# A message-passing kernel: an intermediate goes through DRAM and comes back repeated, two blocks later

## What is computed

```python
s1 = concat(x[src][:, :8], x[dst][:, :8]);  v1 = the 16 vectors of both ends
w  = relu(emb @ fc1_w1 / sqrt(10)) @ fc1_w2 / 4          # 512 weights per edge
s_t, v_t = first layer of s1, v1 with w                  # 8 + 24 values: "v" below
w2 = relu(emb @ fc2_w1 / sqrt(10)) @ fc2_w2 / 4          # 384 weights per edge
scal, gates, vecs = second layer of s_t, v_t with w2
edge_out = concat(tanh(scal), vecs * tanh(gates)) * norm
x = layernorm(x + segment_sum(edge_out, dst))
```

## Time and profile before

| | |
|---|---|
| median of 3 runs | 751.27 us (750.43 to 751.88) |
| the profiled execution | 750.24 us, span from first to last instruction 748.4 us |
| PE busy | 690.1 us (92%) |
| PEld busy | 285.0 us (38%) |
| DVE busy | 691.3 us (92%) |
| ACT busy | 558.7 us (75%) |
| POOL busy | 529.2 us (71%) |
| mean granted clock of TensorE | 0.991 |
| DMA | 28.49 MB, mean 38 GB/s |

### The profile page before, as it was taken

The page is one execution under the profiler, slowest core; times in us unless marked ns, Lnnn a source line. Parts: engine busy times, 40 slices in busy tenths (PEclk is TensorE's granted clock), DMA queues, the critical chain, the costliest instruction groups (busy, mean ns, idle before and its releaser), DMA issues.

```text
span 748.4 us, 19329 instructions
## 1 busy us (share of the span) xinstructions
PE 690.1 (92%) x5998; PEld 285.0 (38%) x5998; DVE 691.3 (92%) x1230; ACT 558.7 (75%) x1279; POOL 529.2 (71%) x656
## 2 busy tenths in 40 slices
PE   0578999999999999999999999999999999999963
PEld 0323434444443443444444344444444444444321
DVE  7578999999999999999999999999999999999983
ACT  2257778887788888877888888888888878788741
POOL 5678787778876887688768876888688877886100
PEclk9999999999999999999999999999999999999997
DMA  4332211121111111121112111211121111111000
GB/s 111 77 91 48 44 31 29 40 46 27 28 42 45 31 28 43 26 46 29 42 26 48 31 42 25 45 29 44 26 48 29 31 36 37 28 27 28 12 1 23
DMA packets 45714, 28.49 MB, mean 38 GB/s; under 512 B 23191, under 2 KB 43833, under 8 KB 45613
## 3 DMA queue, kind: packets, MB, share of 16 engines
q1 hardware_dynamic: 31175, 19.22, 9.8%
q0 software_dynamic: 13312, 6.84, 6.2%
q10 hardware_dynamic: 1126, 1.18, 0.6%
HBM read 22.46 MB, written 4.74 MB: 36 GB/s over the span
## 4 chain that ended last, share of the span: by engine, by line
PE 86%; DVE 5%; issue 2%; ACT 1%; DMA 1%; POOL 0%; DVEq 0%; ACTq 0%
PE ps L1039 15%; PE ps L959 14%; PE ps L977 13%; PE ps L966 9%; PE ps L1019 8%; PE ps L947 6%; PE ps L995 5%; PE ps L1032 4%; PE ps L1026 3%; PE ps L937 3%; DVE p_s L732 3%; PE ps L1007 3%; PE ps L921 2%; PE ps L987 2%; DVE z_s L770 1%
## 5 line engine op out<-in xcount | busy, mean ns | idle before, releaser
L362 POOL DMA_INDIRECT xs<-in_xp,src_i x416 | 401.7, 966 | 114.2 <-issue 104.1
L732 DVE TENSOR_TENSOR p_s<-ps,h 128x2048 f32<-128x2048 f32 x104 | 238.2, 2291 | 20.7 <-PE ps L1039 19.1
L770 DVE TENSOR_TENSOR z_s<-ps,h 128x2048 f32<-128x2048 f32 x104 | 237.6, 2284 | 1.0 <-PE ps L995 1.0
L517 ACT CAST v_s<-ps 128x512 bf16<-128x512 f32 x312 | 182.3, 584 | 48.7 <-PE ps L959 43.6
L1039 PE MATMUL ps<-f,w_f 32*128 32x512 f32 x832 | 120.4, 646 | 4.3
L977 PE MATMUL ps<-z_s,w_z 128*32 128x512 f32 x832 | 110.8, 605 | 2.5 <-DVE z_s L770 2.5
L959 PE MATMUL ps<-p_s,sum_m 128*32 128x512 f32 x832 | 111.8, 606 | 0.2
L483 ACT COPY f<-ps 128x512 f32<-128x512 f32 x104 | 60.9, 586 | 41.8 <-PE ps L947 41.8
L966 PE MATMUL ps<-v_s,less 128*128 128x512 bf16 x208 | 81.1, 390 | 2.3 <-ACT v_s L517 2.1
L1019 PEld LDWEIGHTS ps<-ident,u 128*128 128x128 f32 x416 | 43.8, 141 | 86.7 <-issue 86.7
L523 ACT ACTIVATE h<-ps 128x512 f32<-128x512 f32 x104 | 62.1, 597 | 19.7 <-PE ps L1026 12.4
(11 more groups left out here) (129 smaller groups left out, 847.4 us busy)
## 6 DMA issues: line engine op xcount, KB each, us to landing
emb<-e_dram SPq DMA_DIRECT2D x309, 30.0 KB
xs<-in_xp,src_i POOLq DMA_INDIRECT x416
e_dram<-e_part SPq DMA_DIRECT2D x7, 360.0 KB
e_in<-in_emb SPq DMA_DIRECT2D x8, 240.0 KB, 2.9
window<-x_dram SPq DMA_DIRECT2D x104, 7.9 KB
x_dram<-eo_all SPq DMA_DIRECT2D x1, 585.9 KB
eo_all<-in_vec_t SPq DMA_DIRECT2D x1, 528.0 KB, 4.2
place_dram<-eo_all SPq DMA_DIRECT2D x1, 520.0 KB
```

The lines of the kernel that those rows point to most:

```text
L362: nc.gpsimd.indirect_dma_start(xs_r[n][:, t, :], None, xp, bass.IndirectOffsetOnAxis(src_i[:, m * T + t:m * T + t + 1], axis=0)).then_inc( ...
L517: nc.scalar.copy(v_s[:], v_ps).then_inc(v_step, 1)
L732: nc.vector.tensor_tensor(p_s[:], ps[:, 0:4, :], h1_r[m % 2][:].unsqueeze(1).to_broadcast([128, 4, BE]), ALU.mult).then_inc(p_done, 1)
L770: nc.vector.tensor_tensor(z_s[:], ps[:, 0:4, :], h2_r[k % 3][:].unsqueeze(1).to_broadcast([128, 4, BE]), ALU.mult).then_inc(z_done, 1)
```

## The change

v is summed once, in f32, and copied once by ScalarE (`copy_v`). ScalarE stores the 32 rows that differ to DRAM (`store_v`), and SP loads them back with every row repeated 16 times (`load_repeated`, 128 rows of 8 KB), for `products2` two blocks after `products`. The bf16 parts, their subtraction and `repeat` are gone. `sum_m` now holds each column four times, so that row 4c of each group is channel c. `products2` reads the hidden units from PSUM, takes the maximum with zero and multiplies in one instruction; the scale 1/sqrt(10) is in the weights. The order of the loops of TensorE, ScalarE and VectorE is new, and the last blocks run in the loop, which is four steps longer. `emb` has five buffers instead of three. In the fill the loads and stores of 125 rows go in two stripes of 112 and 13 rows (also the output), and casts, constants and the zeroing of `acc` are in another order.

The core of the diff:

```diff
+STRIPES = ((0, 112), (112, P))
+ER = 5
+        v_dram = nc.dram_tensor("v_dram", (NB, 8, 4, BE), F32, kind="Internal").ap()
-        oht_ps = ps[0:WIN * PARTS, 6, :]
+        oht_ps = ps[0:WIN * PARTS, 5, :]
-        STEPS = range(-5, NB + 1)
+        STEPS = range(-5, NB + 5)
...
+            def load_repeated(k):                                            # SP
+                sp.wait_ge(v_stored[k % 2], 16 * (k // 2 + 1))
+                if k >= 2:
+                    sp.wait_ge(z_done, k - 1)
+                sp.dma_start(rep_r[k % 2][:], v_dram[k:k + 1].to_broadcast([16, 8, 4, BE])
+                             ).then_inc(rep_loaded[k % 2], 16)
...
+            for top, bottom in STRIPES:
+                sp.dma_start(x_dram[0:N, :, :].rearrange("(p m) n c -> p m n c", p=P)[top:bottom], x_part[top:bottom]
+                             ).then_inc(x_stored, 16)
...
             for i in STEPS:                                                  # SP
+                if real(i):
+                    load_repeated(i)
                 if real(i + 5) and i + 5 >= 4:
                     load_window(i + 5)
...
-                if real(i + 3) and i + 3 >= 3:
-                    load_emb(i + 3)
+                if real(i + 4) and i >= 0:
+                    load_emb(i + 4)
...
+            def copy_v(m):                                                   # ScalarE
+                act.wait_ge(s1_done, m + 1)
+                if m >= 2:
+                    act.wait_ge(v_stored[m % 2], 16 * (m // 2))
+                nc.scalar.copy(v_r[m % 2][:], v_ps).then_inc(v_copied, 1)
+
+            def store_v(m):
+                act.wait_ge(v_copied, m + 1)
+                act.dma_start(v_dram[m].rearrange("c g e -> g c e"), v_r[m % 2][0:128:4, :]).then_inc(v_stored[m % 2], 16)
...
             for i in STEPS:                                                  # ScalarE, the new loop
+                copy_v(i); tanhs(i - 4); store_v(i); copy_oht(i + 4); copy_sources(i + 3); copy_rows(i + 3)
+                copy_one_hot(i + 4); copy_u(i - 2); copy_f(i + 2); hidden_1(i + 2)
...
             def products2(k):                                                # VectorE
-                dve.wait_ge(rep_done, k + 1)
-                dve.wait_ge(h2_ready, k + 1)
-                nc.vector.tensor_tensor(z_s[:], ps[:, 0:4, :], h2_r[k % 3][:].unsqueeze(1).to_broadcast([128, 4, BE]),
-                                        ALU.mult).then_inc(z_done, 1)
+                dve.wait_ge(h2_done, k + 1)
+                dve.wait_ge(rep_loaded[k % 2], 16 * (k // 2 + 1))
+                nc.vector.scalar_tensor_tensor(out=z_s[:], in0=h2_ps.unsqueeze(1).to_broadcast([128, 4, BE]), scalar=0.0,
+                                               in1=rep_r[k % 2][:], op0=ALU.max, op1=ALU.mult).then_inc(z_done, 1)
...
             for i in STEPS:                                                  # VectorE
                 if real(i):
                     products(i)
+                if real(i - 4):
+                    gate_sums(i - 4)
+                if real(i - 2):
+                    products2(i - 2)
+                if real(i + 2):
+                    sum_along(i + 2)
                 if real(i - 3):
                     gates(i - 3)
-                if real(i - 1):
-                    products2(i - 1)
                 if real(i - 5):
                     base = base_of(i - 5)
+                    accumulate(i - 5, base)
                 if real(i - 4):
                     gated(i - 4)
-                if real(i - 5):
-                    accumulate(i - 5, base)
-                if real(i - 3):
-                    gate_sums(i - 3)
-                if real(i - 4):
                     outputs(i - 4)
-                if real(i + 2):
-                    sum_along(i + 2)
...
-                for step, at_step in enumerate((0, 1, 3, 4, 5, 6, 7, 8)):
+                for step, at_step in enumerate((-2, -2, 0, 0, 0, 1, 1, 1)):
...
+            def turn(k):                                                     # TensorE
+                pe.wait_ge(u_ready, k + 1)
+                pe.wait_ge(v_copied, min(k + 4, NB))
...
+            def over_nodes(k):
+                pe.wait_ge(eo_done, k + 1)
+                pe.wait_ge(z_done, min(k + 4, NB))
...
             for i in STEPS:                                                  # TensorE, the new loop
+                sum_1(i); first_layer(i + 1); spread_places(i + 4); turn(i - 3); spread_edges(i + 4); rows(i + 3)
+                over_nodes(i - 5); sum_2(i - 2); turn_features(i + 2); hidden_2(i - 1); hidden_1(i + 2)
```

More of the change, by code:

```diff
@@ L100, in program @@
         oht_r = [sb(f"oht{n}", [WIN * PARTS, BE], BF16) for n in range(2)]
-        emb_r = [sb(f"emb{n}", [96, BE], BF16) for n in range(3)]
+        emb_r = [sb(f"emb{n}", [96, BE], BF16) for n in range(ER)]
         e_in = sb("e_in", [SB * HID, BE])
@@ L108, in program @@
         h1_r = [sb(f"h1_{n}", [128, BE]) for n in range(2)]
-        h2_r = [sb(f"h2_{n}", [128, BE]) for n in range(3)]
         p_s = sb("p_s", [128, 4, BE])
@@ L349, in _ @@
             first, end = HALVES[0]
-            sp.dma_start(out.rearrange("(p m) d -> p m d", p=P)[:, first:end, :], yn[0:P, first:end, :]).then_inc(stored, 16)
-            sp.wait_ge(stored, 32)
+            for top, bottom in STRIPES:
+                sp.dma_start(out.rearrange("(p m) d -> p m d", p=P)[top:bottom, first:end, :], yn[top:bottom, first:end, :]
+                             ).then_inc(stored, 16)
+            sp.wait_ge(stored, 64)
         @block.gpsimd
@@ L416, in _ @@
             nc.gpsimd.memset(place_part[:, 3:KP, :], 1.0).then_inc(place_step, 1)
-            for n in range(3):
-                nc.gpsimd.memset(emb_r[n][:], 0.0).then_inc(emb_zeroed, 1)
             pool.wait_ge(src_loaded, 16)
@@ L566, in _ @@
             copy_oht(0)
+            copy_one_hot(0)
             act.wait_ge(emb_zeroed, 1)
@@ L611, in _ @@
             act.wait_ge(y_ready, 2)
-            act.dma_start(out.rearrange("(p m) d -> p m d", p=P)[:, first:end, :], yn[0:P, first:end, :]).then_inc(stored, 16)
+            for top, bottom in STRIPES:
+                act.dma_start(out.rearrange("(p m) d -> p m d", p=P)[top:bottom, first:end, :], yn[top:bottom, first:end, :]
+                              ).then_inc(stored, 16)
         @block.vector
@@ L650, in _ @@
             setup[0] += 1
+            for n in range(ER):
+                last = nc.vector.memset(emb_r[n][:], 0.0)
+            last.then_inc(emb_zeroed, 1)
             dve.wait_ge(pool_consts, 5)
@@ L939, in spread_edges, with rows @@
                 last.then_inc(ohs_spread, 1)
+            def rows(m):
+                pe.wait_ge(window_loaded[m % 3], 16 * (m // 3 + 1))
+                pe.wait_ge(oht_copied, m + 1)
+                if m + 1 >= NB:
+                    pe.wait_ge(f_copied, m - 1)
+                for t in range(T):
+                    last = nc.tensor.matmul(rows_ps[:, t, :], oht_r[m % 2][:, TE * t:TE * t + TE], window_r[m % 3][:],
+                                            start=True, stop=True)
+                last.then_inc(rows_done, 1)
             def turn_features(m):
@@ L979, in sum_2 @@
                 last.then_inc(s2_done, 1)
-            def over_nodes(k):
-                pe.wait_ge(eo_done, k + 1)
-                if k + 6 > NB:
-                    pe.wait_ge(acc_done, k)
-                pe.wait_ge(h2_ready, min(k + 6, NB))
-                for t in range(T):
-                    last = nc.tensor.matmul(node_ps[32 * t:32 * t + 32], eo_all[:, k, t, 8:OC], ohs_r[k % OH][:, t, :],
-                                            start=True, stop=True)
-                last.then_inc(node_done, 1)
@@ L1043, in misfits_of_all @@
+            def hidden_2(m):
+                if m >= 4:
+                    pe.wait_ge(acc_done, m - 3)
+                elif m >= 1:
+                    pe.wait_ge(z_done, m)
+                nc.tensor.matmul(h2_ps, w_first[:, 1, :], emb_r[m % ER][:], start=True, stop=True).then_inc(h2_done, 1)
             def misfits_of_all():
@@ L1060, in _ @@
                 if i == -4:
-                    spread_places(0)
-                if real(i - 1):
-                    repeat(i - 1)
-                if real(i):
-                    hidden_2(i)
+                    misfits_of_all()
+                if i == -1:
+                    pe.wait_ge(weights_ready, 3)
                 if real(i):
                     sum_1(i)
-                if real(i - 5):
-                    over_nodes(i - 5)
+                if real(i + 1):
+                    first_layer(i + 1)
+                if real(i + 4):
+                    spread_places(i + 4)
+                if real(i - 3):
+                    turn(i - 3)
                 if real(i + 4):
```

345 lines of the change are left out of this document (133 added, 212 removed).

## The result

The changed kernel takes 882.24 us (median of 4 runs, 879.95 to 885.28) against 750.91 for the kernel before beside it: 1.175 times as long, interval 1.1711 to 1.1789. I had forecast 771 and a range of 730 to 790. The direction was right, the size was not: instead of 21 us it lost 131.

The account below looks back on a forecast made before the run. TensorE was taken to set the pace, VectorE 0.2 us behind; after the change VectorE's 6.64 plus 0.14 gives 6.78 us per block. Fill 68.9, blocks 664.4 and drain 35.2 make span 768.5, so 771 us; range 730 to 790.

Parts of the forecast that it names:

- rival (c): TensorE's clock falls because it rests about 1.4 us per block, or a load needs over 9 us: 785 to 830, chance 0.15.
- VectorE alone, 6.64: VectorE's own work per block without waits: 6.23 us, plus 0.12 for a dependency and 0.29 for the register load.
- It hides: v's store and repeated load through DRAM never delay VectorE: load 4.0 us plus 2 latency, under about 9 us of cover.
- The price of the second product with the maximum: `products2` on VectorE, now with a maximum in front, priced at 2.21 us like both large products, bounds -0.05 and +0.1.
- The register load: `base_of` on VectorE, now between `gates` and `accumulate`, is exposed: 0.94 instead of 0.65 us, +0.29 per block, bounds 0 and +0.4.
- rival (a): VectorE's register load hides after all, as before the change: 729 to 743 us, faster; chance 0.20.
- The dependency of `outputs`: On VectorE `outputs` now directly follows `gated`, whose result it needs: +0.12 us per block.
- The chain through TensorE, +0.14: Matmuls from a product to `gates` take 5.18 to 5.32 us against VectorE's 5.18; excess taken as 0.14 per block.
- my own sign of being wrong: The forecast is wrong if `accumulate` starts within 0.7 us of `gates`' first instruction, or the clock is below 0.97.
- Fill, -7: Before the sixth product: 7 us gained, bounds 0 and 12.5, with x's store and windows some 5 us less in stripes.
- Drain, +1.5: From the last product to the end: 33.66 us before grows by 1.5, bounds -2 and +6.5.
- Sum: Whole kernel: sixth product at 68.9, blocks 664.4, drain 35.2, so span 768.5 and 771 us; 758 to 785 had chance 0.60.

Follow-up runs that it names:

- f1: Changed kernel, but from block 2 on the load of the repeated v brings 16 of 128 rows (wrong result); 849.52 us, 1.132 of the kernel before.
- f2: Changed kernel, but v is stored for blocks 0 and 1 only, with full loads of those kept (wrong result); 845.70 us, 1.1269 of the kernel before.
- h2: h1 with GpSimd's two products of the directions cut to 128x8 from block 4 on; 970.72 us on a chip where the kernel before takes 992.4.
- i1: h2 run once more on a chip where the kernel before takes 987.14 us; 972.73 us, 0.985 of the kernel before.
- h1: g1 with five idle matmuls per block instead of nine; 969.53 us, 0.973 of the kernel before, on a chip where that takes 992.4.
- a1: The changed kernel itself, unedited, as the reference; 881.84 us beside 750.35 for the kernel before.
- g1: f1 and f3 in one: changed kernel with the short load and nine idle matmuls per block; 844.54 us, 1.1256 of the kernel before.
- g3: f2 and f3 in one: changed kernel without v's store from block 2 on, with nine idle matmuls per block; 851.71 us, 1.1352 of the kernel before.
- w1_stripes: The kernel before with only the change's stripes in x's load and store and the output's stores; 745.49 us, 0.9941 of the kernel before.
- f3: Changed kernel with nine idle TensorE matmuls per block in its waiting time, DMAs unchanged; 883.39 us, 1.1771 of the kernel before.

## Why the prediction was right or wrong

Three steps of the sum failed. By size: the low clock, which the sum put at nothing and left to rival (c), cost 40 us; "VectorE alone, 6.64" was 0.35 us per block too small, mostly because `outputs` now meets GpSimd's products, 34 us; and "It hides" was false for v's trip through DRAM, 26 us in the blocks and some 5 in the fill and the drain. The direction was right, and not by luck: a block without the trip's wait and without a fall of the clock still takes 7.13 us, over the 6.52 before.

The account (the profiled execution took 879.95 us), with f1 and f2 as the measure of a block without the DMA's wait (mean 7.54, middle 7.13):

| | us per block | us in all |
|---|---|---|
| forecast | 6.78 | 771 |
| VectorE's own order, 7.13 - 6.78 | 0.35 | 34 |
| falls of the clock, 7.54 - 7.13 | 0.41 | 40 |
| wait for v's trip, 7.80 - 7.54 | 0.26 | 26 |
| fill, 75.16 - 68.9 | | 6 |
| drain, 38.1 - 35.2 | | 3 |
| sum | 7.80 | 880 |

The first and third rows of loss rest on runs (h2 and i1 against h1 for 0.21 of the 0.35; f1, f2 against a1 for the trip). For the second, runs show that the long blocks go when the clock is held (g1 against f1, g3 against f2). Its 40 us are the mean less the middle of f1 and f2: no run has the blocks at 7.13 with the clock held, because a kernel that keeps it at no cost of its own was tried (h1) but ran only where it could not be read. The rows add up to the measured time because they are taken from it; they are a division of the loss, and a cure of one cause need not give back just its row.

**VectorE alone, 6.64.** The price of the second product with the maximum was right: 2287 ns on average, 2284 before. The register load was right in kind: it is exposed in nearly every block, and rival (a), that it hides, falls. Its place was mis-sized by little: from the first of `gates` to `accumulate` 1.05 us, where I had 0.94. The dependency of `outputs` cost its 0.12 (0.29 from `gated` to `outputs`, I had 0.26). The sum held for rows of before, but a step was missing: I took the small instructions' lengths from the kernel before and moved them without asking what GpSimd does at their new place. That is +0.22 between `outputs` and the next product, the largest part of the 0.35.

**The chain through TensorE, +0.14.** Right. In f1's 7.13 us block `gates` starts 0.44 after `sum_along` where 0.28 was VectorE's own: 0.16. The pitch from `sum_1` to `first_layer` is 1.00 there (411.91 to 412.91 on TensorE's timeline of f1), as I had chosen.

**The repeat through DRAM, "it hides".** This is the step whose argument failed outright. Where the load lay on the chain that ended last it took 7.1 to 8.3 us (in a1 up to 12.6), not 6: its megabyte went at about 136 GB/s (1.05 MB in 7.74 us), where the earlier trace rows show 259 at the same DMA share. And I had counted the store as being over by the end of step i, 6.8 us after the product's start; it took 5.2 to 7.8 us on that chain, about 2.9 of them due to the previous load, which I had not put in its way at all. In the chain shown it was over after 11.4 us. So of the 16.2 us that two blocks leave, the load had 4.8 and not my 9, and it needed 7.7. The short load gave back 29.6 us of the profiled execution (f1's span is 848.5 us): 25 in the blocks, 2.8 in the fill, 1.9 in the drain. The 2 us of latency in my 6 were an estimate for which the forecast had no row; on the page of the kernel before loads of 160 and 240 KB land 2.3 and 2.9 us after their issue.

**Rival (c), the clock.** That the clock falls behind a rest was right: in f1's block above TensorE had rested 1.86 us, and from 405 to 411 us the granted clock reads 0.50. The forecast had the chain's matmuls double there; the eight of `sum_2` (L991) take 1.93 us in the fall and 1.04 in the next block. Its price came out right in part by luck, for the share of blocks was a guess: I had one block in five at 2.2 us, 43 us in all. f1 has 23 of 98 intervals over 8.2 us, 1.5 us longer than 7.13 on average, which is 35 us, and 14 more at about 7.6, which I can't put down to one cause. Its range, 785 to 830, was too low for 882 as well, and my own sign of being wrong, a clock below 0.97, was there. The earlier trace rows had shown a fall to 0.55 behind 1.63 us of rest in two, and my own sum had 1.4 us of rest in each block. A rest of that size, which the forecast itself calls for in every block, should not have had 0.15; I took the forecast's figure for the block and then treated the fall that it implies as another case. The granted clock in the loop was 0.90, mixed from stretches at 1.00 (390 to 420 us) and at 0.50 (433 to 439 us).

**Fill, -7.** Only 0.75 was left. The 5 us that I had given the stripes, with the transfer at the 259 GB/s of the earlier trace rows, are a term that no run shows: in `w1_stripes`, which has nothing else of the change, the windows start 3.4 us earlier and the sixth product 2.45. The first product came 4.4 us earlier (33.66 against 38.04), the second only at 45.74 (46.45 before). The late constants (`acc` zeroed, 2.73 us) and the second part of the directions (a reciprocal of 2.35 and two products) stand between the two on VectorE; I had listed them against the gain, and gave them too little. In the kernel before the reciprocal (2.34 us) stands at 66.11, and `acc` is zeroed at 18.1. Besides, 2.8 us of the 6.3 that I missed are the trip of v: the wait at 71.00 above, and f1's sixth product comes at 72.40 for 75.16.

**Drain, +1.5.** It was +4.4, within the bounds that I gave. The granted clock from 840 us on is 0.68, where the kernel before has 0.84 in its drain (`sum_1` takes 1.98 us, 1.06 before), and VectorE waits 2.36 us for the last block's load, for which the forecast had the two trips in the drain but no wait.

**Sum.** Every term that missed did so to the same side, and the range, with a load too slow or a clock too low as one rival, had no case in which both happened. They aren't independent: f3 shows that with the clock at 0.99 VectorE waits for the load more often, 56 times against 36. That the waits for the load in turn cost clock is plausible, but the granted clock hardly shows it (0.90 and 0.92 with them, 0.92 and 0.93 without).

## What to carry to other kernels

When an instruction is moved, read at its new place what the other engines do there; a length from the old place may hold only beside the old neighbours (`outputs` took 0.28 us there and 0.51 beside GpSimd's products). A round trip through DRAM is the time until the data is there to be stored, the store, the load (4.1, 7.3 and 7.7 us in the chain above), and what each may lose to the other's last turn; add them from one common start before saying that the trip hides. And where a plan leaves TensorE idle in every block, and the trace shows the clock falling behind a rest (to 0.55 in the earlier trace rows), the low clock belongs to the forecast itself, not to the rivals.

## What the hardware showed that I had not expected

- VectorE instructions with two SBUF inputs took 0.51 (`outputs`) and 0.53 us (`gated`) instead of 0.28 and 0.22 beside GpSimd's tensor products of 0.51 us each, and 0.29 and 0.22 with these cut to 128x8. In the blocks shown they ended 0.07 to 0.16 us after GpSimd's instruction did.
- One load of 128 rows of 8 KB that repeat the same 64 KB took 7.1 to 8.3 us in the changed kernel's profile, with the DMA engines 75% busy. Why it stays near 136 GB/s isn't settled.
- Nine idle matmuls a block kept the granted clock at 0.99 in f3 and 1.00 in g1 from 120 to 800 us (0.92 in a1 and f1, without them), but those that still ran when the chain's next matmul was ready held it back by 0.4 us a block in g1.
- On three chips the kernel before took 982 to 992 us instead of 750, and there the changed kernel with the short load was 0.973 of it instead of 1.132. The granted clock of the kernel before was 0.88 to 0.92 there instead of 0.98 to 0.99. What bounds a kernel on such a chip is open.
